# Spatial product of a frequency-routed convolution block: kept pixel-major and added in front of the last projection, star scale folded away

## The chip, the cores and the metric

One Trainium2 chip, one of its cores. The metric is the device time of one execution in microseconds. The kernel before took 259.8 us in the median of three runs (259.14 to 264.2).

## What is computed

The input `x` is 32 images of 128 channels and 16x16 pixels, in fp32. A first block multiplies each image's channels by a gate (a small spline network on the channel means). The second block is the one that the change touches. For each image, with z the normalised input:

```python
xp = star_scale * jnp.square(jax.nn.relu(einsum(z, w_pw1))) + star_bias      # pixels x 256
xf = jnp.fft.rfft2(xp)
weight = einsum('bfc,hwf->bhwc', routeing, cw)                   # per image and channel, complex
spatial_weight = einsum('bfc,hwf->bhwc', spatial_routeing, spatial_weights)
xs = jnp.fft.irfft2(xf * weight)
out = xp * spatial_weight + xs
x = x + einsum('bhwm,dm->bhwd', out, w_pw2)
```

`routeing` and `spatial_routeing` are softmaxes over four filters; their logits come from two small convolution branches over z, averaged over the pixels. The transform is done with matmuls: a 128-slot real form of the spectrum, whose even and odd rows see only the sum and the difference of the upper and lower half of the pixels ("folding").

## The kernel before, in words

Everything is written out by hand, engine by engine, with semaphores. PE is TensorE, DVE VectorE, ACT ScalarE, POOL GpSimd, SP the DMA queue. The first 90 us load, normalise and run the branch convolutions (`taps`, L1198), which PE fills. Then comes the image loop, 32 rounds, one image each, with the second half's softmax work laid in between its rounds 0 to 9 (`windows`, `image_sums`, `logits`, `centred`, `routing`, `routing_part`). The end of `windows` and of `image_sums` is followed at once by the next round's first DVE instruction, L988.

What one image i goes through, with the line of the profile:

- PE `expand`: six f16 matmuls into `bank[0]` (L1292). ACT: relu (L584) and square (L588) into `sq_v`. DVE `halves`: scale and bias into `xp` (L988, 128x512), then its even sum and odd difference into the one buffer `eo` (L994, L995, 128x256 each).
- PE `waves_of`: four fp32 matmuls of `eo` with `forward` into `bank[2]` (L1305, 128 columns each; the trace counts two passes of each). ACT copies them to `spec` (L594).
- PE `mix`: four bf16 matmuls of 32 rows that make the slot filter (`bank[4]`) and the pixel filter (`bank[3]`) of the image (L1334). ACT copies the pixel filter to `swt` (L600).
- PE `turn_pixels`: four fp32 transposes of `xp` to channel-major, into `bank[5]` (in the trace L1106, the line of the helper `turn`). DVE `spatial`: `qt` = `bank[5]` times `swt` (L1014).
- DVE `terms`: `spec` times the slot filter, into `t_re` and `t_im` (L1005, L1006 and the small L1007). POOL `products`: their difference and sum into `prod` (L420, L421, 128x256 each).
- PE `reduce`: four fp32 matmuls of `prod` with `pw2_t` (L1359); ACT copies to `y_sb` (L612). PE `compose`: two fp32 matmuls of `qt` with `pw2_t`, 256 columns each, into `bank[6]` (L1371), then two of `y_sb` with `inverse` (L1378); ACT copies these to `folded` in two instructions (L618, L620).
- POOL `unfold`: sum and difference of `folded` into `waves` (L430, L431), then `waves` added to `x_all` (L436). DVE `finish`: `x_all` times its coefficient plus `bank[6]` (L1018). SP stores the image.

The order of a round is fixed on every engine. PE in round i: expand(i+2), waves_of(i+1), turn_pixels(i+1), mix(i+1), every second round `turn_route` (L1348), reduce(i), compose(i). DVE: halves(i+2), terms(i+1), spatial(i+1), finish(i). POOL: products(i), unfold(i-1), with a wait in `unfold` that looks a round ahead on another engine:

```python
                pool.wait_ge(folded_ready, 2 * i + 2)
                if ahead:
                    pool.wait_ge(eo_ready, 2 * i + 8)
```

So POOL begins image i's `waves` only after DVE has written `eo` of image i+3. The last image is treated apart: DVE itself makes its products (L1090, L1091), and its spatial and spectral parts are added up in `bank[6]` before one last add (L1098).

Of the kernel before, what the change touches and what calls it, by code (L numbers as in the profile page):

```python
# [40 lines left out]
P = 128  # L41
# [121 lines left out]
def build(nc, x, early, kan2, later, sym, branch_r, branch_s, out):  # L163
    ctx = ExitStack()
    with ctx:
# [17 lines left out]
        def of(tensor, pack, name):  # L183
# [77 lines left out]
        relu_v, sq_v = (sb(name, [P, 512])[:, :] for name in ("relu_v", "sq_v"))  # L261

        route = sb("route", [P, 2, P], BF16)
        eo, swt, qt = (sb(name, [P, 2, 256])[:, :, :] for name in ("eo", "swt", "qt"))
        xp = [sb(f"xp{n}", [P, 2, 256])[:, :, :] for n in range(2)]
# [6 lines left out]
        t_last = z32[:, :, :].rearrange("p k s -> p (k s)").rearrange("p (c m a s) -> p c m a s", c=2, m=2, a=2)  # L272

        bank = [ps(f"bank{n}", [P, 512])[:, :] for n in range(8)]
        mixed_slot = bank[4].rearrange("p (m a s) -> p m a s", m=2, a=2)
        mixed_pixel = bank[3].rearrange("p (m s) -> p m s", m=2)
# [24 lines left out]
        v_done, relu_ready, sq_ready, xp_ready, eo_ready = (sem(n) for n in (  # L301
            "v_done", "relu_ready", "sq_ready", "xp_ready", "eo_ready"))
        dft_done, xt_done, w_done, spec_ready, sw_ready = (sem(n) for n in (
            "dft_done", "xt_done", "w_done", "spec_ready", "sw_ready"))
        terms_ready, prod_ready, qt_ready, y_done, y_ready = (sem(n) for n in (
            "terms_ready", "prod_ready", "qt_ready", "y_done", "y_ready"))
        inverse_ready, x_scaled, last_ready = sem("inverse_ready"), sem("x_scaled"), sem("last_ready")
        sp_done, sp_added, folded_done, folded_ready, waves_ready, fin_ready, stored = (sem(n) for n in (
            "sp_done", "sp_added", "folded_done", "folded_ready", "waves_ready", "fin_ready", "stored"))
# [51 lines left out]
        def _(pool):  # L361
# [12 lines left out]
            pool.memset(unused, 0.0).then_inc(rt_zeroed, 1)  # L374
            def places(half, layer):
# [24 lines left out]
            steps.then(pool.tensor_copy(f_res[:, 2:4, :], sw_nat))  # L400
# [14 lines left out]
            def products(i):  # L415
                pool.wait_ge(terms_ready, 3 * i + 3)
# [6 lines left out]
            def unfold(i, ahead=True, between=None):  # L423

                pool.wait_ge(folded_ready, 2 * i + 2)
                if ahead:
                    pool.wait_ge(eo_ready, 2 * i + 8)
# [4 lines left out]
                if between:  # L432
                    between()
# [19 lines left out]
        def _(act):  # L453
# [189 lines left out]
            def round_of(i, pair, j, between=None):  # L643
# [3 lines left out]
                if j == 0:  # L647
                    route_copy(pair + 1)
# [877 lines left out]
```

## Time and profile before

| | |
|---|---|
| Median of three runs | 259.8 us (259.14 to 264.2) |
| Span of the profiled execution, first to last instruction | 257.2 us |
| Granted TensorE clock over the span | 1.000 |
| PE busy | 240.7 us, 94% of the span |
| DVE busy | 194.2 us, 76% |
| ACT busy | 161.1 us, 63% |
| POOL busy | 108.9 us, 42% |
| DMA, mean over the span | 51 GB/s |

The page gives the profiled execution by its span, 257.2 us; its own time is not listed apart, so the 2.6 us up to the median stand for what lies around the span. Of the chain of waits that ended last, 70% is PE and 11% DVE. All times below are microseconds from the span's start. On DVE and POOL an instruction can start before the record of the one ahead has ended; the step from start to start is then what the engine spends on it, and the full duration counts only where somebody waits for the result. DMA issues lie in the first 15 us and, one store an image, in the loop.

### The profile page before, as it was taken

What the parts mean: (1) busy time and instruction counts of PE and PEld (TensorE: products, weight loads), DVE (VectorE), ACT (ScalarE), POOL (GpSimd) and SP (SyncE); (2) the same over time, 40 slices, a digit from 0 to 9 for tenths busy, and PEclk for the clock granted to TensorE, in tenths of its full rate; (3) what the DMA queues carried; (4) which work ended last, traced back from release to release, by engine and by line L of the source; (5) the groups of instructions that cost most, each with busy time, mean ns of one, the idle gap of its engine ahead of it and who ended that gap; (6) DMA issues with size and microseconds to landing.
All of it is one profiled execution on the core that took longest, in us unless ns stands there. A gap on an engine that the chain in (4) does not pass through costs nothing.

```text
span 257.2 us, 6874 instructions
## 1 busy us (share of the span) xinstructions
PE 240.7 (94%) x2225; PEld 187.7 (73%) x2225; DVE 194.2 (76%) x548; ACT 161.1 (63%) x380; POOL 108.9 (42%) x197
## 2 busy tenths in 40 slices
PE   0697799999999999999999999999999999999995
PEld 0686765554545555886988889988888888888984
DVE  3988999955939626996779998858767768768773
ACT  2034586645976748755676677676676676676772
POOL 2422440120000002257455665765665665665663
PEclk9999999999999999999999999999999999999999
DMA  7999200000000000001010010010010010010002
GB/s 212 364 326 348 105 3 3 1 4 3 0 3 0 3 0 0 4 23 35 9 43 20 23 42 24 20 43 20 20 43 20 20 41 20 20 41 20 23 20 82
DMA packets 9483, 13.19 MB, mean 51 GB/s; under 512 B 732, under 2 KB 8924, under 8 KB 9332
## 3 DMA queue, kind: packets, MB, share of 16 engines
q1 hardware_dynamic: 9428, 12.80, 15.3%
q8 instruction: 15, 0.25, 0.4%
q10 hardware_dynamic: 32, 0.08, 0.2%
q14 instruction: 8, 0.07, 0.1%
HBM read 8.69 MB, written 4.19 MB: 50 GB/s over the span
## 4 chain that ended last, share of the span: by engine, by line
PE 70%; DVE 11%; issue 8%; POOL 4%; DMA 3%; ACT 2%; SPq 1%; POOLq 0%; DVEq 0%; ACTq 0%
PE bank L1198 19%; PE bank L1359 10%; PE bank L1305 8%; PE bank L1371 8%; PE bank L1292 6%; PE bank L1106 4%; PE bank L1378 4%; PE bank L1334 3%; DMA x_all<-in_x 3%; PE bank L1136 1%; POOL prod L421 1%; PE bank L1263 1%; PE bank L1213 1%; PE bank L1348 1%; DVE stats L726 1%
## 5 line engine op out<-in xcount | busy, mean ns | idle before, releaser
L420 POOL TENSOR_TENSOR prod<-t_re,t_im 128x256 f32<-128x256 f32 x31 | 22.6, 729 | 51.6 <-DVE t_re L1007 51.2
L988 DVE TENSOR_SCALAR xp<-sq_v,later_sb 128x512 f32<-128x512 f32 x32 | 17.6, 550 | 32.2 <-ACT sq_v L588 31.9
L1198 PE MATMUL bank<-z_all,split_h 128*64 128x450 f16 (+2 forms) x320 | 37.4, 374 | 1.0 <-ACT z_all L503 1.0
L1359 PE MATMUL bank<-later_sb,prod 128*128 128x128 f32 x256 | 36.3, 285 | 0.2 <-POOL prod L421 0.2
L430 POOL TENSOR_TENSOR waves<-folded 128x128 f32<-128x128 f32 x31 | 14.1, 455 | 51.1 <-DVE eo L995 47.4
L1305 PE MATMUL bank<-later_sb,eo 128*128 128x128 f32 x256 | 34.2, 276 | 0.4 <-DVE eo L994 0.4
L1359 PEld LDWEIGHTS bank<-later_sb,prod 128*128 128x128 f32 x256 | 31.1, 192 | 3.9 <-POOL prod L421 2.3
L1305 PEld LDWEIGHTS bank<-later_sb,eo 128*128 128x128 f32 x256 | 31.1, 192 | 1.5 <-DVE eo L994 0.7
L1371 PE MATMUL bank<-qt,later_sb 128*128 128x256 f32 x124 | 31.9, 380 | 0.0
L618 ACT ACTIVATE folded<-bank,coef 128x128 f32<-128x128 f32 x31 | 11.4, 367 | 32.5 <-PE bank L1378 26.2
L1198 PEld LDWEIGHTS bank<-z_all,split_h 128*64 128x64 f16 x320 | 17.2, 110 | 16.0 <-issue 3.1
L436 POOL TENSOR_TENSOR x_all<-x_all,waves 128x256 f32 (+1 forms) x31 | 22.6, 728 | 5.8 <-POOL waves L431 4.9
L584 ACT ACTIVATE relu_v<-bank,w_max 128x512 f32<-128x512 f32 x32 | 22.0, 688 | 3.7 <-PE bank L1292 2.6
L1136 PE MATMUL bank<-early_sb 128*128 128x128 f32 x102 | 15.0, 305 | 9.0 <-DMA x_all<-in_x 9.0
L1014 DVE TENSOR_TENSOR qt<-bank,swt 128x512 f32<-128x512 f32 x31 | 21.2, 683 | 2.7 <-PE bank L1371 2.5
L421 POOL TENSOR_TENSOR prod<-t_re,t_im 128x256 f32<-128x256 f32 x31 | 22.8, 734 | 0.0
L1292 PE MATMUL bank<-split_h,z_all 128*128 128x256 f16 x128 | 22.7, 273 | 0.0
L1371 PEld LDWEIGHTS bank<-qt,later_sb 128*128 128x128 f32 x124 | 21.2, 191 | 1.6
L588 ACT ACTIVATE sq_v<-relu_v 128x512 f32<-128x512 f32 x32 | 20.2, 631 | 1.0
L1005 DVE TENSOR_TENSOR t_re<-spec,bank 128x504 f32<-128x504 f32 x31 | 20.8, 671 | 0.0
L1006 DVE TENSOR_TENSOR t_im<-spec,bank 128x504 f32<-128x504 f32 x31 | 20.8, 671 | 0.0
L1136 PEld LDWEIGHTS bank<-early_sb 128*128 128x128 f32 x102 | 13.6, 214 | 9.0 <-issue 9.0
(176 smaller groups left out, 495.2 us busy)
## 6 DMA issues: line engine op xcount, KB each, us to landing
x_all<-in_x SPq DMA_DIRECT2D x8, 512.0 KB, 8.6
out<-x_all SPq DMA_DIRECT2D x32, 128.0 KB, 1.7
sp_t<-in_branch_s SPq DMA_DIRECT2D x1, 2560.0 KB, 15.6
later_sb<-in_later SPq DMA_DIRECT2D x1, 918.5 KB, 8.8
sym_all<-in_sym SPq DMA_DIRECT2D x1, 292.5 KB
early_sb<-in_early SPq DMA_DIRECT2D x1, 278.0 KB, 3.6
rwf_t<-in_branch_r SPq DMA_DIRECT2D x1, 256.0 KB, 11.8
kan_sb<-in_kan ACTq DMA_DIRECT2D x1, 80.8 KB, 3.3
```

The costliest lines, as they stand in the source:

```text
L420: pool.tensor_tensor(prod[:, :, :, 0, :], halved[0][:, :, 0], halved[1][:, :, 1], ALU.subtract).then_inc(prod_ready, 1)
L421: pool.tensor_tensor(prod[:, :, :, 1, :], halved[0][:, :, 1], halved[1][:, :, 0], ALU.add).then_inc(prod_ready, 1)
L436: pool.tensor_tensor(one(x_all, i), one(x_all, i), waves[:, :, :].rearrange("p u s -> p (u s)"), ALU.add).then_inc(fin_ready, 1)
L584: act.activation(relu_v[:, :], bank[0], ACT.Relu, scale=w_max[:, 2:3]).then_inc(relu_ready, 1)
L1005: tt(t_re[:, :, :, 2:P], spec[:, :, :, 2:P], mixed_slot[:, :, 0, 2:P].unsqueeze(2).broadcast_to(wide_shape), ALU.mult).then_inc(terms_read ...
L1014: tt(qt[:, :, :], bank[5].rearrange("p (m s) -> p m s", m=2), swt[:, :, :], ALU.mult).then_inc(qt_ready, 1)
L1136: mm(bank[1][:, 0:P], group, ident, start=True, stop=True)
L1198: last = mm(dst[:, :, rows_out, cols_out], w[:, t, :], pixels(z_all[:, b:b + 2, part, :])[:, :, rows_in, cols_in], start=(n == 0 and t in ...
L1292: last = mm(bank[0][:, t * MED:(t + 1) * MED], z[:, part, cols], w, start=(n == 0), stop=(n == 2))
L1305: last = mm(dst[:, m, :, 64 * odd:64 * odd + 64], eo[:, odd, m * P:(m + 1) * P], forward[:, odd, :, :], start=True, stop=True)
L1359: last = mm(bank[1][:, odd * C:(odd + 1) * C], prod[:, m, odd].rearrange("p a s -> p (a s)"), pw2_t[:, m, :], start=(m == 0), stop=(m == 1))
L1371: last = mm(bank[6][:, 0:HW], pw2_t[:, m, :], qt[:, m, :], start=(m == 0), stop=(m == 1))
```

## The change

1. The product `qt` is made pixel-major: DVE multiplies `xp` (as written, plus a bias) by a pixel filter that `mix` now makes pixel-major, in `bank[4]`, read from PSUM. The four transposes (`turn_pixels`), ACT's copy to `swt`, and the two 256-column matmuls of `compose` are gone.
2. POOL folds `qt` (`fold`: sum and difference into `qt_eo`), PE transforms it with four fp32 matmuls of 128 columns into `bank[5]` (`waves_onto`), and DVE adds `bank[5]` to POOL's `prod` (`add_pixels`) before `reduce`.
3. The final sum is DVE's alone: `finish` adds `waves` to `x_all`; POOL's L436 is gone, and so is the wait `ahead`.
4. The scale is folded: its root goes into ACT's relu scale, its sign into the filters; ACT's square writes `xp` directly, the bias goes into DVE's two instructions, and L988 is gone. `eo` has two buffers.
5. The orders of all four engines are new; `expand` runs three images ahead, `finish` one round behind. The last image runs like the others.

```diff
             def products(i):
-                pool.wait_ge(terms_ready, 3 * i + 3)
+                pool.wait_ge(re_ready, 2 * i + 2)
+                pool.wait_ge(im_ready, i + 1)
...
-            def unfold(i, ahead=True, between=None):
-
+            def fold(i):
+                pool.wait_ge(qt_ready, i + 1)
+                if not isinstance(i, int) or i >= 1:
+                    pool.wait_ge(q_done, i)
+                pool.tensor_tensor(qt_eo[:, 0, :], qt[:, 0, :], qt[:, 1, :], ALU.add).then_inc(q_folded, 1)
+                pool.tensor_tensor(qt_eo[:, 1, :], qt[:, 0, :], qt[:, 1, :], ALU.subtract).then_inc(q_folded, 1)
+
+            def unfold(i):
                 pool.wait_ge(folded_ready, 2 * i + 2)
-                if ahead:
-                    pool.wait_ge(eo_ready, 2 * i + 8)
                 if not isinstance(i, int) or i >= 1:
                     pool.wait_ge(fin_ready, i)
...
-                pool.tensor_tensor(one(x_all, i), one(x_all, i), waves[:, :, :].rearrange("p u s -> p (u s)"), ALU.add).then_inc(fin_ready, 1)
...
+            with pool.Fori(1, NB - 2) as i:
+                unfold(i)
+                fold(i + 2)
+                products(i + 2)
...
+            def square(i, p):
                 act.wait_ge(relu_ready, i + 1)
-                if not isinstance(i, int) or i >= 1:
-                    act.wait_ge(xp_ready, i)
-                act.activation(sq_v[:, :], relu_v[:, :], ACT.Square).then_inc(sq_ready, 1)
+                if not isinstance(i, int) or i >= 2:
+                    act.wait_ge(qt_ready, i - 1)
+                    act.wait_ge(odd_ready, i - 1)
+                act.activation(xp[p].rearrange("p t m -> p (t m)"), relu_v[:, :], ACT.Square).then_inc(sq_ready, 1)
...
             def round_of(i, pair, j, between=None):
-                relu_square(i + 2)
                 spectrum(i + 1)
-                spatial_mix(i + 1)
                 if j == 0:
                     route_copy(pair + 1)
+                y_copy(i)
                 if between:
                     between()
-                y_copy(i)
+                rectified(i + 3)
                 folded_copy(i)
...
+                square(i + 3, 1 - j)
...
+            def even_sum(i, p):
                 dve.wait_ge(sq_ready, i + 1)
...
+                dve.scalar_tensor_tensor(out=eo[p][:, 0, :], in0=xp[p][:, 0, :], scalar=shift_2[:, 0:1], in1=xp[p][:, 1, :],
+                                         op0=ALU.add, op1=ALU.add).then_inc(even_ready, 1)
+                tt(eo[p][:, 1, :], xp[p][:, 0, :], xp[p][:, 1, :], ALU.subtract).then_inc(odd_ready, 1)
+
+            def spatial(i, p):
+                dve.wait_ge(pixel_done, i + 1)
+                if not isinstance(i, int) or i >= 1:
+                    dve.wait_ge(q_folded, 2 * i)
+                dve.scalar_tensor_tensor(out=qt[:, :, :], in0=xp[p], scalar=shift[:, 0:1], in1=mixed_pixel,
+                                         op0=ALU.add, op1=ALU.mult).then_inc(qt_ready, 1)
...
+            def add_pixels(i):
+                dve.wait_ge(q_done, i + 1)
+                dve.wait_ge(prod_ready, 2 * i + 2)
+                flat = prod[:, :, :, :, :].rearrange("p m o a s -> p (m o a s)")
+                tt(flat, flat, bank[5], ALU.add).then_inc(total_ready, 1)
...
             def finish(i):
-                dve.wait_ge(sp_done, i + 1)
+                dve.wait_ge(waves_ready, 2 * i + 2)
...
-            def round_of(i, p):
-                halves(i + 2, p)
+            def round_of(i, p, between=None):
+                add_pixels(i)
+                even_sum(i + 2, p)
+                spatial(i + 1, 1 - p)
+                if between:
+                    between()
                 terms(i + 1)
-                spatial(i + 1)
-                finish(i)
+                if not isinstance(i, int) or i >= 1:
+                    finish(i - 1)
...
+            def waves_onto(i):
...
+                for odd in range(2):
+                    pe.wait_ge(q_folded, 2 * i + 1 + odd)
+                    for m in range(2):
+                        last = mm(bank[5][:, (2 * m + odd) * P:(2 * m + odd + 1) * P], qt_eo[:, odd, m * P:(m + 1) * P], forward[:, odd, :, :],
+                                  start=True, stop=True)
+                last.then_inc(q_done, 1)
...
             def reduce(i):
...
-                pe.wait_ge(prod_ready, 2 * i + 2)
+                pe.wait_ge(total_ready, i + 1)
...
+                waves_onto(i)
+                if not isinstance(i, int) or i >= 1:
+                    waves_of(i + 1, 1 - j)
                 mix(i + 1, pair + j, 1 - j)
                 if j == 0:
                     turn_route(pair + 1, half)
...
                 reduce(i)
...
+                expand(i + 3)
+                if not between:
+                    compose(i, pair + 2)
```

How the order of instructions moves, at the two places that matter. First POOL, two images of the loop before; L420 and L421 are `products`, L430 and L431 the `waves` of `unfold`, L436 its add to `x_all`:

```order
L420 TENSOR_TENSOR prod<-t_re,t_im 128x4x64
L421 TENSOR_TENSOR prod<-t_re,t_im 128x4x64
L425 ISA
L427 REGISTER_ALU
L430 TENSOR_TENSOR waves<-folded 128x128
L431 TENSOR_TENSOR waves<-folded 128x128
L436 ISA
L436 TENSOR_TENSOR x_all<-x_all,waves 128x256
```

And POOL's whole loop body after, one image (L438 and L439 are `fold`, in front of the products):

```order
L445 TENSOR_TENSOR waves<-folded 128x128
L446 TENSOR_TENSOR waves<-folded 128x128
L435 REGISTER_ALU
L437 REGISTER_ALU
L438 TENSOR_TENSOR qt_eo<-qt 128x256
L439 TENSOR_TENSOR qt_eo<-qt 128x256
L426 ISA
L431 TENSOR_TENSOR prod<-t_re,t_im 128x4x64
L432 TENSOR_TENSOR prod<-t_re,t_im 128x4x64
L455 REGISTER_ALU
L455 COMPARE_AND_BRANCH
```

The add to `x_all` has left POOL, and two folds of 256 columns stand between an image's `waves` and the next products. Next DVE, one image of the loop before:

```order
L988 TENSOR_SCALAR xp0<-sq_v,later_sb 128x512
L994 TENSOR_TENSOR eo<-xp0 128x256
L995 TENSOR_TENSOR eo<-xp0 128x256
L1005 TENSOR_TENSOR t_re<-spec,bank4 128x4x126
L1006 TENSOR_TENSOR t_im<-spec,bank4 128x4x126
L1007 TENSOR_TENSOR t_re<-spec,bank4 128x4x2
L1014 TENSOR_TENSOR qt<-bank5,swt 128x512
L1018 SCALAR_TENSOR_TENSOR x_all<-x_all,coef,bank6 128x256
```

And one image of DVE's loop after, beginning with `add_pixels` (L1027):

```order
L1027 TENSOR_TENSOR prod<-prod,bank5 128x512
L1001 SCALAR_TENSOR_TENSOR eo1<-xp1,shift_2 128x256
L1003 TENSOR_TENSOR eo1<-xp1 128x256
L1009 SCALAR_TENSOR_TENSOR qt<-xp0,shift,bank4 128x512
L1019 TENSOR_TENSOR t_re<-spec,bank3 128x4x126
L1020 TENSOR_TENSOR t_re<-spec,bank3 128x4x2
L1021 TENSOR_TENSOR t_im<-spec,bank3 128x4x126
L1031 SCALAR_TENSOR_TENSOR x_all<-x_all,coef,waves 128x256
```

The first instruction now reads what POOL makes of the instructions above it in the round before; the spatial product stands ahead of the terms, and `finish` reads both inputs from SBUF where it read one from PSUM.

## Rows read from the trace of the kernel before

**Rows 1.** Page, busy time: engine, microseconds, share of the span, instructions.

```profile
PE 240.7 (94%) x2225; PEld 187.7 (73%) x2225; DVE 194.2 (76%) x548; ACT 161.1 (63%) x380; POOL 108.9 (42%) x197
```

**Rows 2.** Timeline, DVE `finish` of images 10 and 28 (start, duration, engine, line).

```profile
157.23 0.47 DVE L1018 SCALAR_TENSOR_TENSOR x_all<-x_all,coef,bank 128x256 f32<-128x256 f32 x1
...
243.55 0.47 DVE L1018 SCALAR_TENSOR_TENSOR x_all<-x_all,coef,bank 128x256 f32 x1
```

**Rows 3.** Timeline, PE in one round of the loop.

```profile
209.23 0.38 PE L1292 MATMUL bank<-split_h,z_all 128*128 128x256 f16 x2
...
209.88 1.06 PE L1305 MATMUL bank<-later_sb,eo 128*128 128x128 f32 x8
210.78 0.60 PE L1106 MATMUL bank<-early_sb,xp 128*128 128x128 f32 x4
211.31 0.39 PE L1334 MATMUL bank<-filters,route 32*128 32x256 bf16 x4
...
212.75 1.03 PE L1371 MATMUL bank<-qt,later_sb 128*128 128x256 f32 x4
213.62 0.64 PE L1378 MATMUL bank<-later_sb,y_sb 128*128 128x128 f32 x4
```

**Rows 4.** Timeline, DVE in one round of the loop.

```profile
207.44 0.43 DVE L994 TENSOR_TENSOR eo<-xp 128x256 f32<-128x256 f32 x1
207.78 0.42 DVE L995 TENSOR_TENSOR eo<-xp 128x256 f32<-128x256 f32 x1
208.12 0.67 DVE L1005 TENSOR_TENSOR t_re<-spec,bank 128x504 f32<-128x504 f32 x1
...
208.71 0.67 DVE L1006 TENSOR_TENSOR t_im<-spec,bank 128x504 f32<-128x504 f32 x1
...
209.30 0.15 DVE L1007 TENSOR_TENSOR t_re<-spec,bank 128x8 f32<-128x8 f32 x1
...
209.37 0.68 DVE L1014 TENSOR_TENSOR qt<-bank,swt 128x512 f32<-128x512 f32 x1
...
209.97 0.47 DVE L1018 SCALAR_TENSOR_TENSOR x_all<-x_all,coef,bank 128x256 f32 x1
```

**Rows 5.** Timeline, POOL in the loop, and the DVE instruction that released it.

```profile
213.24 0.45 POOL L430 TENSOR_TENSOR waves<-folded 128x128 f32<-128x128 f32 x1 [1.80 <-DVE eo L995]
...
247.54 0.15 DVE L1007 TENSOR_TENSOR t_re<-spec,bank 128x8 f32<-128x8 f32 x1
247.78 0.72 POOL L420 TENSOR_TENSOR prod<-t_re,t_im 128x256 f32<-128x256 f32 x1 [0.33 <-DVE t_re L1007]
...
248.46 0.73 POOL L421 TENSOR_TENSOR prod<-t_re,t_im 128x256 f32<-128x256 f32 x1
```

**Rows 6.** Timeline, places where DVE and POOL both read SBUF.

```profile
44.66 0.49 POOL L383 TENSOR_TENSOR k_rel<-k_dist,k_inv 128x176 f32<-128x176 f32 x1 [9.36 <-DVE k_dist L781]
44.85 0.51 DVE L785 SCALAR_TENSOR_TENSOR k_bas<-k_dist,k_ge 128x176 f32<-128x176 f32 x1
...
106.12 0.74 POOL L421 TENSOR_TENSOR prod<-t_re,t_im 128x256 f32<-128x256 f32 x1
106.26 0.62 DVE L890 TENSOR_TENSOR win<-win,cols_sum 128x8 f32<-128x8 f32 x1
```

**Rows 7.** Groups by shape, POOL: count, busy us, mean ns of one.

```profile
L383 POOL TENSOR_TENSOR k_rel<-k_dist,k_inv 128x160 f32<-128x160 f32 x2 | 1.1, 554 | 0.0
```

**Rows 8.** Timeline, PE and DVE where the loop begins and where it ends.

```profile
98.27 0.39 PE L1334 MATMUL bank<-filters,route 32*128 32x256 bf16 x4
...
104.02 0.67 DVE L1005 TENSOR_TENSOR t_re<-spec,bank 128x504 f32<-128x504 f32 x1
...
246.37 0.67 DVE L1005 TENSOR_TENSOR t_re<-spec,bank 128x504 f32<-128x504 f32 x1
...
254.60 0.42 DVE L1098 TENSOR_TENSOR x_all<-x_all,bank 128x256 f32<-128x256 f32 x1 [2.09 <-PE bank L1468]
```

**Rows 9.** Timeline, the first DVE instruction behind `windows`.

```profile
107.80 0.54 DVE L988 TENSOR_SCALAR xp<-sq_v,later_sb 128x512 f32<-128x512 f32 x1
```

More of the change, by code:

```diff
@@ L374, in _ @@
             pool.memset(unused, 0.0).then_inc(rt_zeroed, 1)
+            pool.wait_ge(in_later, 16)
+            steps.then(pool.tensor_scalar(sign_01[:, :], star[:, 0:1], 0.0, None, ALU.is_ge))
+            pool.tensor_scalar(sign[:, :], sign_01[:, :], 2.0, -1.0, ALU.mult, ALU.add).then_inc(sign_set, 1)
+            pool.wait_ge(sign_set, 1)
+            pool.tensor_tensor(size[:, :], star[:, 0:1], sign[:, :], ALU.mult).then_inc(sign_set, 1)
+            steps.then(pool.tensor_tensor(shift[:, :], star[:, 1:2], sign[:, :], ALU.mult))
+            pool.tensor_scalar(shift_2[:, :], shift[:, :], 2.0, None, ALU.mult).then_inc(sign_set, 1)
             def places(half, layer):
@@ L399, in _ @@
             pool.wait_ge(in_later, 16)
-            steps.then(pool.tensor_copy(f_res[:, 2:4, :], sw_nat))
+            pool.wait_ge(sign_set, 1)
+            steps.then(pool.tensor_scalar(f_res[:, 2:4, :], sw_nat, sign[:, 0:1], None, ALU.mult))
             for part in range(3):
@@ L494, in _ @@
             sigmoid_sum(0, 1)
-            ahead(ACT.Sqrt)
+            act.wait_ge(sign_set, 2)
+            act.activation(root[:, :], size[:, :], ACT.Sqrt).then_inc(root_set, 1)
             deviation(0, 2)
@@ L1048, in _ @@
             round_of(3, 1)
-            halves(6, 0)
-            logits(1)
-            terms(5)
-            spatial(5)
-            finish(4)
+            round_of(4, 0, lambda: logits(1))
             centred(1)
@@ L1327, in mix @@
+                last.then_inc(q_done, 1)
+            def mix(i, pair, j, branches=(0, 1)):
                 pe.wait_ge(rt_out, pair + 1)
                 if not isinstance(i, int) or i >= 1:
[L1329 to L1335 removed]
@@ L1338, in turn_route @@
+                if 0 in branches:
+                    pixel.then_inc(pixel_done, 1)
+                if 1 in branches:
+                    slot.then_inc(slot_done, 1)
             def turn_route(n, half):
@@ L1363, in compose @@
             def compose(i, turned_routes):
-                pe.wait_ge(qt_ready, i + 1)
-                if isinstance(i, int) and i == 3:
-                    pe.wait_ge(copied, 3)
-                if not isinstance(i, int) or i >= 1:
-                    pe.wait_ge(sp_added, i)
-                for m in range(2):
-                    last = mm(bank[6][:, 0:HW], pw2_t[:, m, :], qt[:, m, :], start=(m == 0), stop=(m == 1))
-                last.then_inc(sp_done, 1)
                 pe.wait_ge(y_ready, i + 1)
@@ L1398, in _ @@
             expand(1)
+            mix(0, 0, 0, (0,))
             taps(7, 2, 5)
```

322 lines of the change are left out of this document (125 added, 197 removed).

## The prediction

> **What bounds the kernel now.** I read first the page's busy times. The reader should see one engine that is nearly always at work: PE with 94% of the span, against 76% for DVE, 63% for ACT and 42% for POOL [rows 1]. The branch convolutions ahead of the image loop are not touched, so the question is the length of a round. Between the `finish` of image 10 and that of image 28 lie 18 rounds in 86.32 us [rows 2], which is 4.80 us a round. PE's rows of one round follow on one another without a hole [rows 3]: PE sets 4.80. The other engines wait for it once a round.
>
> Two durations matter later. On DVE the reader should look at steps from start to start: 0.34 for a sum of 256 columns, 0.59 for one of 504, 0.60 for one of 512 with an input in PSUM, whose full duration is 0.68 [rows 4]. On POOL a two-input instruction of 256 columns lasts 0.73 and the next one starts 0.68 after it; one of 128 columns lasts 0.45 [rows 5]. DVE's last term ends at 247.69 and POOL starts at 247.78, so a release costs 0.09 [rows 5].
>
> **PE's part of the change.** The four transposes go: from 210.78 to 211.31, 0.53. The two wide matmuls of `compose` go: from 212.75 to 213.62, 0.87. `waves_onto` comes, four fp32 matmuls of 128 columns just like `waves_of`, which take 209.88 to 210.78, 0.90 [rows 3]. The mix keeps its four matmuls of 256 columns. PE's work falls by 0.50, to 4.30 us a round. ACT loses its copy to `swt` and waited for PE anyway, so that is worth nothing by itself, nor is the gone L988: DVE was idle beside it.
>
> **What is late next.** The change closes a ring between DVE and POOL that was not there. DVE, in order, does add_pixels(i), two halves, spatial(i+1), terms(i+1), finish(i-1), and then add_pixels(i+1). That last one waits for POOL's products(i+1), and in POOL's order these stand behind fold(i+1), which waits for DVE's spatial(i+1). So a round cannot be shorter than this path, step by step:
>
> - add_pixels, 512 columns from SBUF and PSUM, start to start 0.60 as L1014 to L1018 [rows 4];
> - the even sum 0.36 and the odd difference 0.34. The odd one is L995. The even one has the three-operand form, which the trace shows only with PSUM: 0.47 against 0.42 for the plain form [rows 4]. Bounds 0.34 and 0.39;
> - the spatial product to its end, 0.73: 0.68 as L1014, and 0.05 for its three-operand form. Bounds 0.68 and 0.78, since this form at 512 columns is in no row;
> - the release to POOL, 0.09;
> - two folds and two products of 256 columns, three steps of 0.68 and one full 0.73, together 2.77 [rows 5];
> - the release from POOL to DVE, in no row; 0.06, between 0 and 0.1.
>
> The sum is 4.95. A second path over terms(i+1) instead of the folds is shorter: spatial 0.60 from start to start, terms 0.59, 0.07 and 0.67, release 0.09, products 1.41, release 0.06, with the 1.30 ahead of them 4.79. POOL's own work is only some 3.6 a round, so neither engine looks full; it is the alternation that costs. PE, 4.30, gets holes.
>
> **What the two engines do to each other.** In the rows of the spline layer both read SBUF together. POOL's L383 runs 44.66 to 45.15; DVE's L785, two inputs in SBUF, starts at 44.85 and takes 0.51 [rows 6], ending 0.21 behind POOL's end, which is about its 176 columns at one each 1.04 ns (0.60 minus 0.34 over 256 columns, [rows 4]). It stood until POOL was done. L890, with 8 columns, takes 0.62 and ends at 106.88, when POOL's L421 has ended at 106.86 [rows 6]. POOL pays less: its next L383, of only 160 columns, lasts 0.55 where the 176-column one took 0.49 [rows 6, 7], some 0.10 too long by its size, that is DVE's 0.18 of reading less a start-up of 0.08. Now `finish` reads `x_all` and `waves`, both in SBUF (before, one was in PSUM), and it is issued some 3.2 after add_pixels starts, in the middle of the folds and products that the ring runs through. By the same measure 256 columns hold POOL for 0.27 less 0.08, 0.19. The halves fall beside the end of the waves (L445, L446), worth 0.01 or so. I take 0.20: a round of 5.15. Bounds are 0 and the whole 0.47 of `finish`.
>
> The Trainium skill says more on this (SBUF — State Buffer, Who interferes with whom): a VectorE instruction with two SBUF inputs and a GpSimd instruction that reads SBUF shut each other out, and the second to issue is blocked until the first has finished. On DVE's side the trace agrees (L785, L890); on POOL's side the 0.10 is less than a whole instruction. Taken whole it gives the third case below.
>
> **Sum.** Before, from terms(1) at 104.02 to terms(30) at 246.37 [rows 8], 29 rounds take 142.35, so 3.2 more than 29 times 4.80: the softmax work of the second half. After:
>
> - 29 rounds at 5.15: 149.4.
> - Softmax work: the 3.2 again, since what PE and DVE do there stays (the free 1.3 us of DVE between `finish` and the products hides it as the idle time did before). But `windows`, 1.54 us from 106.26 to 107.80 [rows 6, 9], reads SBUF twice per small instruction and now falls on the folds and products: most of it must stand until POOL is done, some 1.0 late; the same for `image_sums`; four more places at 0.25 each. Together 6.2 (bounds 3.2 and 7.5).
> - Loop: 155.6 against 142.35, +13.2.
> - Start: the slot half of mix(0), at 98.27 [rows 8], now stands behind expand(2), 0.65, and waves_of(1), 0.90 [rows 3], and behind the pixel half issued apart. Terms(1) comes 1.9 later (bounds 1.0 and 2.2).
> - End: before, from terms(30) at 246.37 to the end of the last add, 254.60 plus 0.42, 8.65 [rows 8]; DVE made the last products itself. After, along the ring: terms(30) to add_pixels(30) 3.15, then 0.60 and 0.73 to the end of the last spatial product, 0.09, four POOL instructions 2.77 plus 0.19, release and add_pixels 0.74, then reduce, copy and the last matmuls 2.55 (four matmuls at 128 columns 0.90 as L1305 and two at 256 columns 0.87 as L1371 [rows 3], 0.78 estimated for the copy between and three releases), add 0.47: 11.3. That is +2.6.
>
> The star scale adds five tiny POOL instructions at 14 us and four on DVE near 60 us; POOL waits for DVE at the one place and PE fills the other, so zero, at most 0.5. It all comes to +17.7: a span of 274.9. With the 2.6 outside the span, as before, 277.5 us.
>
> **Rivals.**
>
> 1. The ring without the lock: finish fits between POOL's instructions. 29 times 4.95 and 3.2 is 146.75, +4.4; start 1.9, end 2.4; +8.7: 268.5 us. For it: POOL's solo rows vary by little. Against: L890 and L785 waited.
> 2. The lock taken whole: POOL loses the full 0.47 per round. 5.42 by 29 is 157.2, with 6.2 it is +21.0; start 1.9, end 2.9: 285.6 us. Against it the 0.55 of L383.
> 3. PE stays the bound, and the change pays: 4.30 by 29 is 124.7, with 3.2 it is -14.5, start +1.9, end 0: 247.2 us. For it: PE's 94% and 0.50 less work. It decides as soon as POOL's four instructions take less than 2.77 minus 0.65, 2.12 together (0.53 each), or DVE's order leaves the ring open. Every POOL row of 256 columns says 0.73, and the order is read off the program, so I give it little.
> 4. Every size at its lowest: spatial 0.68, even 0.34, releases 0.07 less, no lock: 4.81 a round, +0.3; start 1.0, end 2.0: 263.1 us, which is no difference.
>
> **How the numbers follow.** Forecast 0.60, rival 1 0.20, rival 2 0.11, rival 3 0.04, rival 4 0.05. The measurement can tell about 2% from no change, 5.2 us, so the border is at 265.0 above and 254.6 below. Forecast, 1 and 2 lie above it, 0.91; of that I move 0.01 to the middle for what I may have left out. Slower 0.90, same 0.06, faster 0.04. The range leaves out rivals 3 and 4 and the upper part of 2: 267 to 286.
>
> **What would show it.** In the profile after: DVE's add_pixels (L1027) idle in front, released by POOL's second product (L432), once a round and about 1.2 long; rounds of about 5.15; PE's share near 85% with holes ahead of L1357 and L1312; L1031 (`finish`) longer than 0.47, because it stands behind a fold; L431 longer than 0.73. If L1031 reads 0.47, it is rival 1; if L431 reads 1.1 and more, rival 2. If rounds measure 4.3 and DVE does not wait for POOL, the ring is wrong and so is the sign.

## The result and the profile after

The changed kernel takes 280.15 us (median, 279.78 to 280.35), the one before, run beside it, 260.06: a ratio of 1.079 (95% interval 1.076 to 1.081). Forecast were 277.5 us and a slower kernel. The span of the profiled execution is 278.2, against 257.2. Executions of one kernel can differ by up to 5 us (259.14 to 264.2 before), so the experiments below are compared by the length of their rounds as well as by their time.

The page of the kernel after: busy times, the chain that ended last by engine, and the two groups of section 5 that matter most.

```profile
PE 247.6 (89%) x2225; PEld 186.3 (67%) x2225; DVE 209.5 (75%) x549; ACT 146.7 (53%) x348; POOL 139.0 (50%) x237
...
PE 51%; DVE 34%; issue 6%; POOL 3%; DMA 2%; ACT 1%; DVEq 1%; POOLq 1%; SPq 0%; ACTq 0%
...
L1357 PE MATMUL bank<-later_sb,prod 128*128 128x128 f32 x256 | 37.4, 290 | 12.7 <-DVE prod L1027 11.8
L1027 DVE TENSOR_TENSOR prod<-prod,bank 128x512 f32<-128x512 f32 x32 | 22.0, 686 | 34.8 <-POOL prod L432 31.9
```

PE has gone from 94% [rows 1] to 89%, and a third of the chain now runs over DVE. The last line is the shape of the answer: `add_pixels` (L1027) stands idle 34.8 us in all, nearly all of it for POOL's second product, L432. No engine is over 90% busy any more, and the kernel takes 20 us more.

One round of the loop on DVE and POOL, after (start, duration, and in brackets the idle time ahead and who ended it). It answers to [rows 4, 5].

```profile
204.58 0.69 DVE L1027 TENSOR_TENSOR prod<-prod,bank 128x512 f32<-128x512 f32 x1 [1.30 <-POOL prod L432]
...
205.19 0.48 DVE L1001 SCALAR_TENSOR_TENSOR eo<-xp,shift 128x256 f32<-128x256 f32 x1
...
205.58 0.41 DVE L1003 TENSOR_TENSOR eo<-xp 128x256 f32<-128x256 f32 x1
205.92 0.74 DVE L1009 SCALAR_TENSOR_TENSOR qt<-xp,shift,bank 128x512 f32<-128x512 f32 x1
206.57 0.67 DVE L1019 TENSOR_TENSOR t_re<-spec,bank 128x504 f32<-128x504 f32 x1
206.81 0.72 POOL L438 TENSOR_TENSOR qt_eo<-qt 128x256 f32<-128x256 f32 x1 [1.44 <-DVE qt L1009]
...
207.50 0.73 POOL L439 TENSOR_TENSOR qt_eo<-qt 128x256 f32<-128x256 f32 x1
207.83 0.69 DVE L1031 SCALAR_TENSOR_TENSOR x_all<-x_all,coef,waves 128x256 f32 x1
208.19 0.91 POOL L431 TENSOR_TENSOR prod<-t_re,t_im 128x256 f32<-128x256 f32 x1
...
209.07 0.71 POOL L432 TENSOR_TENSOR prod<-t_re,t_im 128x256 f32<-128x256 f32 x1
...
209.81 0.69 DVE L1027 TENSOR_TENSOR prod<-prod,bank 128x512 f32<-128x512 f32 x1 [1.30 <-POOL prod L432]
```

Read it as one ring. DVE runs add, halves, spatial product without a gap (204.58 to 206.66), POOL takes over at 206.81 and runs folds and products without a gap to 209.78, DVE starts again at 209.81. Each engine waits about 1.3 to 1.4 for the other, once a round: 5.23 in all. `finish` at 207.83 lies across a fold, lasts 0.69 and not 0.47, and the product behind it (208.19) lasts 0.91 and not 0.73.

### The profile page after: what moved, and what is told of

Same layout as the page of the kernel before. It is cut to its first block, busy times and chain, and to the rows that moved or that the text cites. A ratio compares the mean times of both kernels' runs of the same rounds, so it can differ in the third digit from the quotient of the medians.

```text
span 278.2 us, 6918 instructions
## 1 busy us (share of the span) xinstructions
PE 247.6 (89%) x2225; PEld 186.3 (67%) x2225; DVE 209.5 (75%) x549; ACT 146.7 (53%) x348; POOL 139.0 (50%) x237
## 4 chain that ended last, share of the span: by engine, by line
PE 51%; DVE 34%; issue 6%; POOL 3%; DMA 2%; ACT 1%; DVEq 1%; POOLq 1%; SPq 0%; ACTq 0%
PE bank L1191 18%; PE bank L1357 6%; PE bank L1312 6%; PE bank L1299 5%; DVE qt L1009 4%; DVE t_re L1019 4%; DVE t_im L1021 4%; DVE prod L1027 4%; PE bank L1286 4%; DVE x_all L1031 3%; POOL prod L432 3%; PE bank L1368 3%; DMA x_all<-in_x 2%; DVE eo L1001 2%; PE bank L1326 2%
## 5 line engine op out<-in xcount | busy, mean ns | idle before, releaser
L438 POOL TENSOR_TENSOR qt_eo<-qt 128x256 f32<-128x256 f32 x32 | 23.3, 727 | 94.1 <-DVE qt L1009 94.1
L1357 PE MATMUL bank<-later_sb,prod 128*128 128x128 f32 x256 | 37.4, 290 | 12.7 <-DVE prod L1027 11.8
L1027 DVE TENSOR_TENSOR prod<-prod,bank 128x512 f32<-128x512 f32 x32 | 22.0, 686 | 34.8 <-POOL prod L432 31.9
L1357 PEld LDWEIGHTS bank<-later_sb,prod 128*128 128x128 f32 x256 | 31.3, 192 | 19.2 <-DVE prod L1027 17.4
L1312 PE MATMUL bank<-later_sb,qt_eo 128*128 128x128 f32 x256 | 41.7, 295 | 0.3
L1312 PEld LDWEIGHTS bank<-later_sb,qt_eo 128*128 128x128 f32 x256 | 33.4, 192 | 7.2 <-issue 2.8
L612 ACT ACTIVATE spec<-bank 128x512 f32<-128x512 f32 x32 | 19.1, 598 | 31.7 <-PE bank L1299 31.0
L1299 PE MATMUL bank<-later_sb,eo 128*128 128x128 f32 x256 | 33.9, 275 | 0.0
L625 ACT ACTIVATE y_sb<-bank 128x256 f32<-128x256 f32 x32 | 12.3, 384 | 37.6 <-PE bank L1357 37.6
L1299 PEld LDWEIGHTS bank<-later_sb,eo 128*128 128x128 f32 x256 | 31.1, 192 | 0.4 <-issue 0.4
L431 POOL TENSOR_TENSOR prod<-t_re,t_im 128x256 f32<-128x256 f32 x32 | 28.7, 898 | 2.1 <-DVE t_im L1021 1.3
L598 ACT ACTIVATE relu_v<-bank,relu_scale 128x512 f32<-128x512 f32 x32 | 22.0, 688 | 12.1 <-PE bank L1286 12.1
L1009 DVE SCALAR_TENSOR_TENSOR qt<-xp,shift,bank 128x512 f32<-128x512 f32 x32 | 23.7, 741 | 0.0
L439 POOL TENSOR_TENSOR qt_eo<-qt 128x256 f32<-128x256 f32 x32 | 23.3, 729 | 0.0
L432 POOL TENSOR_TENSOR prod<-t_re,t_im 128x256 f32<-128x256 f32 x32 | 23.2, 724 | 0.0
L1129 PE MATMUL bank<-early_sb 128*128 128x128 f32 x102 | 15.0, 304 | 9.1 <-DMA x_all<-in_x 9.1
L1368 PE MATMUL bank<-later_sb,y_sb 128*128 128x128 f32 x124 | 21.9, 300 | 1.0 <-ACT y_sb L625 0.9
```

The lines of the kernel that those rows point to most:

```text
L431: pool.tensor_tensor(prod[:, :, :, 0, :], halved[0][:, :, 0], halved[1][:, :, 1], ALU.subtract).then_inc(prod_ready, 1)
L432: pool.tensor_tensor(prod[:, :, :, 1, :], halved[0][:, :, 1], halved[1][:, :, 0], ALU.add).then_inc(prod_ready, 1)
L1009: dve.scalar_tensor_tensor(out=qt[:, :, :], in0=xp[p], scalar=shift[:, 0:1], in1=mixed_pixel, op0=ALU.add, op1=ALU.mult).then_inc(qt_ready, 1)
L1027: tt(flat, flat, bank[5], ALU.add).then_inc(total_ready, 1)
L1299: last = mm(dst[:, m, :, 64 * odd:64 * odd + 64], eo[p][:, odd, m * P:(m + 1) * P], forward[:, odd, :, :], start=True, stop=True)
L1312: last = mm(bank[5][:, (2 * m + odd) * P:(2 * m + odd + 1) * P], qt_eo[:, odd, m * P:(m + 1) * P], forward[:, odd, :, :], start=True, stop ...
```

## Experiments

Rounds are counted from one add_pixels to the next, in the rolled loop.

**e1, the lock of `finish`.** From round 10 on `finish` adds a PSUM bank in place of `waves`; the waves are left out of the result.

```diff
-            def finish(i):
+            def finish(i, psum=False):
                 dve.wait_ge(waves_ready, 2 * i + 2)
+                added = bank[6][:, 0:HW] if psum else waves[:, :, :].rearrange("p u s -> p (u s)")
...
-                                         in1=waves[:, :, :].rearrange("p u s -> p (u s)"), op0=ALU.mult, op1=ALU.add).then_inc(fin_ready, 1)
+                                         in1=added, op0=ALU.mult, op1=ALU.add).then_inc(fin_ready, 1)
```

> The changed kernel, but from round 10 on the last sum of each image reads an unused PSUM bank in place of the waves, so it has one SBUF input as before the change; the waves of those images are left out of the result. Lock theory: the first product on GpSimd falls from 0.91 to 0.73, finish from 0.69 to 0.47, and each of some 19 rounds gets 0.2 shorter, 5.23 to 5.03: 276.3 us. Rival (the first product is slow because of its operands or the loop, not because VectorE reads): products and rounds stay, 280 us.

276.07 us, ratio 1.061 (1.058 to 1.064); rounds 5.05 to 5.06. The same place of the round in e1:

```profile
206.34 0.47 DVE L1032 SCALAR_TENSOR_TENSOR x_all<-x_all,coef,bank 128x256 f32 x1
206.70 0.73 POOL L431 TENSOR_TENSOR prod<-t_re,t_im 128x256 f32<-128x256 f32 x1
```

With one of its inputs in PSUM, `finish` takes 0.47 beside a working POOL and POOL's product 0.73. So the 0.22 more on DVE and the 0.18 on POOL come from the second SBUF input, and the round gives back just POOL's part, 0.18. The lock is shown, at the size forecast.

**e2, no folds.** POOL's two folds are left out, and PE transforms the unfolded product. DVE's next spatial product then waits for that transform in place of the folds.

```diff
-                pool.tensor_tensor(qt_eo[:, 0, :], qt[:, 0, :], qt[:, 1, :], ALU.add).then_inc(q_folded, 1)
-                pool.tensor_tensor(qt_eo[:, 1, :], qt[:, 0, :], qt[:, 1, :], ALU.subtract).then_inc(q_folded, 1)
```

> The changed kernel without GpSimd's two folds; TensorE transforms the unfolded halves, so the spatial part of the result is wrong in that it lacks the fold. GpSimd loses 1.38 us of the 3.65 that it works a round. Ring theory: the path over the folds goes, and the next one, over the terms and the products, ends only 0.15 to 0.35 earlier: rounds of 4.9 to 5.1, about 273 us. Rival (rounds are long because GpSimd has more work): the whole 1.38 is saved until TensorE is the bound at 4.4: 254 us.

278.14 us in the median of four (277.88, 278.52, 278.4 and 274.04), where about 273 were expected; rounds 5.02 to 5.03, as expected. Taking 1.4 us of POOL's work out of a round shortens it by only 0.2: the path over the three terms to the two products is next. POOL now waits for the last term:

```profile
207.66 0.67 DVE L1011 TENSOR_TENSOR t_im<-spec,bank 128x504 f32<-128x504 f32 x1
208.25 0.48 DVE L1021 SCALAR_TENSOR_TENSOR x_all<-x_all,coef,waves 128x256 f32 x1
208.41 0.90 POOL L431 TENSOR_TENSOR prod<-t_re,t_im 128x256 f32<-128x256 f32 x1 [2.61 <-DVE t_im L1011]
209.28 0.72 POOL L432 TENSOR_TENSOR prod<-t_re,t_im 128x256 f32<-128x256 f32 x1
...
210.03 0.69 DVE L1017 TENSOR_TENSOR prod<-prod,bank 128x512 f32<-128x512 f32 x1 [1.30 <-POOL prod L432]
```

The span of that profile, 276.0, fell by 2.2 only, where 29 rounds of 0.2 are 6. The rest was lost ahead of the images: its first add_pixels starts at 107.6 and that of the kernel after at 103.98. PE's preparatory 128-column matmuls (`stir`, L1119 here and L1129 there) took longer per piece between 8 and 24 us. First the kernel after, then e2; behind the count stand busy time and mean ns:

```profile
L1129 PE MATMUL bank<-early_sb 128*128 128x128 f32 x66 | 10.2, 316 | 9.1 <-DMA x_all<-in_x 9.1
```

```profile
L1119 PE MATMUL bank<-early_sb 128*128 128x128 f32 x44 | 10.6, 430 | 8.8 <-DMA x_all<-in_x 8.8
```

In both, 16 that follow on one another take some 3.75 at first, 0.23 each; in the kernel after they then fall to half of that, 0.12 (22 in 2.72 from 21.46 us on), and in e2 they still take 0.23 there (16 in 3.62). The execution of 274.04 has a span of 272.1, which is 6.1 under the kernel after, as the rounds say.

**e3, more work for PE.** Four fp32 transposes of 128 columns more a round, ahead of `reduce`, from round 6 on.

```diff
+                    for n in range(4):
+                        turn(bank[6][:, n * P:(n + 1) * P], ident, P)
                 reduce(i)
```

> The changed kernel with four idle fp32 transposes more on TensorE in every round from 6 on, in front of reduce, 0.53 us a round (what the change took away with turn_pixels); the result stays. Ring theory: TensorE has 0.6 to 0.9 of free time a round, so rounds grow by 0 to 0.15: 280 to 284 us. Rival (TensorE still sets the round): 0.53 by 26 rounds, 294 us.

280.1 us (ratio 1.082, 1.074 to 1.091), rounds 5.24. The matmuls are there (92, four a round in 23 rounds, 0.60 to 0.66 each time; for 23 rounds the rival's 294 would be 292), and the hole ahead of `reduce` shrinks from 12.7 to 6.8:

```profile
PE 253.2 (91%) x2317; PEld 194.2 (70%) x2317; DVE 209.3 (75%) x549; ACT 146.8 (53%) x348; POOL 139.3 (50%) x237
...
L1357 PE MATMUL bank<-later_sb,prod 128*128 128x128 f32 x256 | 35.9, 284 | 6.8 <-DVE prod L1027 6.6
```

PE is not the bound, though its share is again 91%. It is not far from it: it has 69% of the chain that ended last, where it had 51%. But as long as the ring is 5.23, the half microsecond a round that the change took from PE buys nothing.

**e8, both costs at once.** e2's edit and e1's together.

```diff
-                pool.tensor_tensor(qt_eo[:, 0, :], qt[:, 0, :], qt[:, 1, :], ALU.add).then_inc(q_folded, 1)
-                pool.tensor_tensor(qt_eo[:, 1, :], qt[:, 0, :], qt[:, 1, :], ALU.subtract).then_inc(q_folded, 1)
...
-                                         in1=waves[:, :, :].rearrange("p u s -> p (u s)"), op0=ALU.mult, op1=ALU.add).then_inc(fin_ready, 1)
+                                         in1=added, op0=ALU.mult, op1=ALU.add).then_inc(fin_ready, 1)
```

> No folds on POOL (PE transforms the unfolded product) and, from round 10 on, finish reads PSUM in place of waves, so both are left out of the result. If the two costs are independent walls on one path, as I now hold: the round without folds was 5.03 because the path then runs over the three terms and the two products, and finish's lock (0.18 on the first product) is still on it. Taking both gives 4.85 a round and about 270 us (274.0 for the run without folds that had the usual start, less 20 rounds of 0.18). Rival: without folds the lock is no longer on the path (finish then falls beside a product that nobody waits for), rounds stay 5.0 and the time stays at 274.

270.9 us, ratio 1.039 (1.036 to 1.042); rounds 4.85 to 4.86, the forecast to 0.01. The two costs add, since e2's ring still has L431 at 0.90 in it and here it is 0.73. Even without folds and lock the ring between DVE and POOL is longer than the 4.80 of before [rows 2].

### Can another order open the ring?

These runs are read by their rounds first, since two things in their profiles lie ahead of the loop's later rounds and lengthen the time without the ring. In e4, e6, e7 and e11 the first add_pixels starts at 107.07 to 108.12, not at 103.98: from 19 to 24 us, 36 to 40 matmuls fill PE's 5 us as in e2, where 44 take 3.57 in the kernel after. And the granted TensorE clock, 1.00 from 160 to 260 us in every run of this part, is lower in some of the rounds with softmax work: 0.83 from 110 to 120, 120 to 130 and 140 to 150 us in e7, for instance. The kernel after has 0.83 from 100 to 110 us only; e1, whose clock is 1.00 there, has the same first round (6.01 for 6.05).

**e4, one image further ahead.** DVE makes the spatial product of image i+2 behind the terms of i+1; PE's mix is split so that its pixel half comes earlier; POOL's folds also wait until DVE's halves of the next image are done.

```diff
                 even_sum(i + 2, p)
-                spatial(i + 1, 1 - p)
...
                 terms(i + 1)
+                spatial(i + 2, p)
...
-            def fold(i):
+            def fold(i, behind=True):
                 pool.wait_ge(qt_ready, i + 1)
+                if behind:
+                    pool.wait_ge(odd_ready, i + 2)
```

> The changed kernel with the spatial product made one image further ahead (same instructions, other order on VectorE and TensorE), and the folds made to wait for the odd difference of the next image. Ring theory: no path goes through spatial product, folds and products in one round any more; what is left is add_pixels, the halves, the folds and the products on GpSimd, 4.5 to 4.65 a round, near TensorE's own 4.4: 260 to 264 us. Rival (the amount of work, not its order, sets the round): 280 us.

272.98 us, ratio 1.048 (1.044 to 1.052), rounds 4.82 and 4.93 in turn. It is 7 us better than the change as it is, and far from the 260 to 264 expected. The spatial product waited for PE's pixel mix (0.40 <-PE), and `finish` behind it (0.80 on average) was still running when the products had ended: add_pixels then waited for its own engine.

**e6, the pixel mix early, and no wait in the folds.**

```diff
                 reduce(i)
+                mix(i + 2, pair + 1, j, (0,))
...
-                    mix(i + 2, pair + 1, j, (0,))
                     compose(i, pair + 2)
...
-                if behind:
-                    pool.wait_ge(odd_ready, i + 2)
```

> The kernel that runs the spatial product an image further ahead, without the wait that held the folds back, and with PE's pixel mix of image i+2 issued right behind reduce(i), ahead of expand and compose. In the run before it (272.98 us, rounds 4.82 to 4.93) the spatial product waited 0.40 for that mix and finish stood in front of add_pixels. If the late mix was the wall, spatial starts 0.4 to 0.5 earlier, and add_pixels then goes by POOL's second product: rounds of 4.6 to 4.7, 266 to 269 us. Rival: finish's lock with the products is the wall whatever the mix does (finish ends when the product ends, as before): rounds stay at 4.8 to 4.9 and the time at 272 to 273.

279.49 us (1.073, 1.067 to 1.079), rounds 4.97: both theories missed it. The rounds are 0.26 shorter than in the kernel after, and the time is not: in the profile, from the first add_pixels to the last are 164.8 us, where it was 168.1, but the first comes 3.8 later. The group of the odd difference, 180 to 260 us (count, busy, mean ns), e6:

```profile
L1003 DVE TENSOR_TENSOR eo<-xp 128x256 f32<-128x256 f32 x17 | 16.1, 949 | 0.0
```

It takes 418 ns in the kernel after. Without the wait the folds run just when DVE makes the halves: the fold L438 stands behind the even sum, and the odd difference behind the fold.

**e7, the transform ahead too.** As e6, and PE's waves_onto(i+1) is issued behind reduce(i); POOL folds before it unfolds.

```diff
             def round_of(i, pair, j, half=0, between=None):
-                waves_onto(i)
...
                 mix(i + 2, pair + 1, j, (0,))
+                waves_onto(i + 1)
```

> As the last, and also the forward transform of the spatial product runs one image ahead: PE issues waves_onto(i+1) behind reduce(i), so waves_of(i+1) opens the round and its spectrum is there when add_pixels(i) ends; POOL folds before it unfolds. Then nothing in the ring between DVE and POOL is longer than add_pixels 0.6, halves 0.7, terms 1.3, products 1.4 and releases 0.2, 4.2 to 4.4 with locks, and PE's own 4.3 is the bound: rounds 4.35 to 4.5 and 256 to 262 us, about the kernel before or a little under it. Rival: DVE is the wall, since its own work with the locks of two halves and finish is some 4.3 to 4.6 a round and the softmax work of the second half no longer finds idle time: rounds 4.6 to 4.7, 264 to 268 us.

286.24 us (1.099, 1.092 to 1.106), rounds 5.23. The collision is plain in its rows:

```profile
209.20 0.72 POOL L438 TENSOR_TENSOR qt_eo<-qt 128x256 f32<-128x256 f32 x1
209.27 0.69 DVE L1027 TENSOR_TENSOR prod<-prod,bank 128x512 f32<-128x512 f32 x1 [0.61 <-POOL prod L432]
...
209.87 1.02 DVE L1001 SCALAR_TENSOR_TENSOR eo<-xp,shift 128x256 f32<-128x256 f32 x1
209.88 0.72 POOL L439 TENSOR_TENSOR qt_eo<-qt 128x256 f32<-128x256 f32 x1
...
210.56 0.64 POOL L445 TENSOR_TENSOR waves<-folded 128x128 f32<-128x128 f32 x1
210.81 0.67 DVE L1003 TENSOR_TENSOR eo<-xp 128x256 f32<-128x256 f32 x1
211.17 0.63 POOL L446 TENSOR_TENSOR waves<-folded 128x128 f32<-128x128 f32 x1
```

add_pixels reads one input from PSUM and takes its 0.69 beside the fold L438. The even sum, with both in SBUF, stands until fold L439 ends at 210.60 and takes another 0.29: 1.02. Reading, it holds up POOL's L445 in turn (0.64 for 0.45), and the odd difference stands until that one ends at 211.20. From add_pixels to the first term are 2.14 (209.27 to 211.41), where 0.60, 0.39 and 0.34 would do: the 0.8 over is what the deeper order had won.

**e9, e7 and `finish` with PSUM.** e7 with e1's edit. Expected was no difference (within 1 us) if PE is the bound there, and rounds 0.1 to 0.2 shorter and 2 to 5 us less if DVE and its locks are the wall. It took 285.72 us (1.100, 1.086 to 1.113), the same time as e7, but the rounds are 5.05 in place of 5.23: the lock of `finish` is on the path there too, at the same 0.18 as in e1, and PE's 4.3 is not the bound. As in e1 the waves are left out of the result. The halves still collide with POOL (0.92 and 0.67). The time does not show the gain, since rounds with softmax work were longer in this profile (8.95, 11.31 and 8.24, in e7 7.08, 10.77 and 6.93). The granted clock was lower there, 0.66 from 120 to 125 us and 0.62 from 143 to 150 (e7: 0.75 from 122 to 127 and 0.72 from 144 to 150); whether that is all of it is open.

**e11, e10, e12, the wait back in.** e11 is e6 and e10 is e7 with this wait and POOL's order as in e4; e12 is e10 with e1's edit.

```diff
-            def fold(i):
+            def fold(i, behind=True):
                 pool.wait_ge(qt_ready, i + 1)
+                if behind:
+                    pool.wait_ge(odd_ready, i + 2)
...
-                fold(i + 2)
                 unfold(i)
+                fold(i + 2)
```

The moved `fold` is e10's alone (e11 has that order already).

> e6_mix_first with the wait put back that holds POOL's folds until DVE's halves of the next image are done. The last call left that wait out, and the trace shows the price: the even sum and the odd difference, two SBUF inputs each, took about 1.0 and 0.67 there instead of 0.4, since each stands until POOL's instruction beside it is finished. With the wait the halves should read 0.6 or less and rounds fall from 4.97 by 0.2 to 0.35, to 4.65 to 4.75: 267 to 271 us. Rival: the order of PE's mix is what cost there, then rounds stay above 4.9.

275.4 us (1.059, 1.055 to 1.064), rounds 4.86 to 4.87. The two durations in the expectation are those of e7; in e6 the even sum took 0.48 and the odd difference 0.95. With the wait they take 0.78 and 0.41: the odd difference is free, and the even sum now stands beside POOL's L448. The wait is worth 0.11 a round where 0.2 to 0.35 were expected, and there is no gain on e4. In its rows the first fold waits 0.78 for the odd difference, and from there POOL runs its four instructions without a gap; the add comes when `finish`, which ended last, is through (e11's two folds, and the spatial product that waits for the second):

```profile
208.29 0.73 POOL L440 TENSOR_TENSOR qt_eo<-qt 128x256 f32<-128x256 f32 x1 [0.78 <-DVE eo L1008]
...
208.98 0.73 POOL L441 TENSOR_TENSOR qt_eo<-qt 128x256 f32<-128x256 f32 x1
...
209.74 0.75 DVE L1014 SCALAR_TENSOR_TENSOR qt<-xp,shift,bank 128x512 f32<-128x512 f32 x1 [0.36 <-POOL qt_eo L441]
...
210.41 0.96 DVE L1036 SCALAR_TENSOR_TENSOR x_all<-x_all,coef,waves 128x256 f32 x1
```

The wait has put the folds between halves and products again: the same ring, closed at another place.

> e7_transform_ahead with the same wait and POOL's order back to waves, folds, products. Theory: SBUF access shared by DVE's two-SBUF instructions and POOL is the real bound now. POOL's six instructions take 3.7 a round and DVE's three (even, odd, finish) can't read meanwhile, 0.27 each by 1.04 ns a column: 4.5 together. Rounds then come to 4.5 to 4.65 against 5.23, and with the softmax rounds still long (10.8 for one there) 262 to 268 us. Rival: the ring itself (not the collisions) is what holds e7 at 5.23: the wait then changes nothing or makes it longer, 284 us and more.

296.3 us (1.139, 1.135 to 1.143), rounds 5.70 and 5.79: the rival, and worse. Here PE's transform waits for the folds (0.46 <-POOL), `expand` stands behind it, ACT's square behind that, and the even sum waits for it (0.96 <-ACT xp). My budget of shared SBUF access (4.5) is a lower limit that no order came near, not a forecast.

> e10 with finish reading PSUM from round 10 on (the waves are left out of the result). By the budget of shared SBUF access it frees 0.2 to 0.27 a round: 0.15 to 0.25 below e10's rounds, 3 to 5 us less, unless PE's own 4.3 is reached first. Rival: no difference from e10, so finish's access is not on the path there.

299.61 us (1.157, 1.149 to 1.164), rounds 5.70 and 5.79 as in e10: `finish` is not on that ring. In the profiles 1.3 us of the difference from e10 lie in one round of the softmax work (7.04 for 5.71), where the granted clock is 0.83 from 150 to 160 us and 1.00 in e10; the rest is open.

**e13, e7 without folds.** e7 with e2's edit.

```diff
-                fold(i + 2)
                 unfold(i)
                 products(i + 2)
```

> e7_transform_ahead without POOL's folds (PE transforms the unfolded product, so the fold is left out of the result). Three orders so far gave rounds of 4.86 to 5.79, all with two folds and two products in a row between DVE's halves and add_pixels. Theory: it is these 1.4 us of folds, by their own time in the ring or by the halves that stand behind them, that no order hides. Without them the halves read 0.4 to 0.7 again and rounds come to 4.3 to 4.6, 22 to 29 rounds of 0.65 to 0.9 less than e7's 286: 262 to 269 us. Rival: e7's order is bad by itself (DVE's own work and the waits for PE), and then rounds stay above 4.9.

278.23 us in the median of six (274.08 to 279.66), rounds 4.73 and 5.02 in turn, 4.87 on average. Taking the folds out is worth 0.36 a round there and not 0.65 to 0.9; in every second round `finish` (0.88) stands behind a product, and the spatial product waits for PE (0.22 and 0.43 in turn). That the folds are all of the cost in the ahead orders is not shown.

No version beat the kernel before. The best that computes the same is e4, 272.98.

## Why the prediction was right, point by point

- **PE loses its place as the bound.** Right: its share is 89% (85% forecast), it has holes ahead of L1357, and e3 shows that work put back costs nothing. The holes forecast ahead of L1312 are not there (0.3 us idle in all). Its eight passes last 1.30 us and more in most rounds, though, where the same shape in L1299 takes 1.06, so part of the wait for the second fold is probably counted as busy.
- **The ring over DVE and POOL.** Right in its order and nearly in every term. Measured: 0.61, 0.39, 0.34, 0.74, release 0.15, folds 0.69 and 0.69, products 0.88 and 0.71, release 0.03, together 5.23; forecast 5.15. The mis-sized terms are the release from DVE to POOL (0.15, I took 0.09), the even sum 0.39 for 0.36, and the POOL steps 0.69 for 0.68; the release back, 0.03, was taken at 0.06. Over 29 rounds the 0.08 are 2.3 of the 3.3 us by which the span was short. DVE's idle time, 1.30, was forecast at 1.2.
- **The second path.** Forecast at 4.79 beside 4.95; e8, without the lock, measures 4.85, 0.06 over; e2, with it, 5.03. Rival 3 had this wrong: faster POOL instructions in the first path alone would not have made PE the bound, since the second path, over terms and products, is longer than 4.30 too. e2 shows it: with no folds at all the round is still 5.03.
- **The lock.** 0.20 forecast, e1 shows 0.18. Rival 1 (none) and rival 2 (the whole 0.47) are both excluded by the rows: L1031 0.69, L431 0.91. The Trainium skill (SBUF — State Buffer, Who interferes with whom) says that the second to issue is blocked until the first has finished. For DVE behind POOL the rows agree (L1001 in e7). For POOL behind DVE they agree as well, once the wait is counted from POOL's own start: `finish` stood until the fold L439 had ended (208.23) and itself ended at 208.52, and the product had started at 208.19, only 0.33 before that. It was 0.18 late. In e2 0.32 of `finish` were left when the product started, and it took 0.90 for 0.73. The clearest case is in e6, where the even sum is not held up itself (0.48) and 0.40 of it are left:

```profile
184.62 0.48 DVE L1001 SCALAR_TENSOR_TENSOR eo<-xp,shift 128x256 f32<-128x256 f32 x1
184.70 0.98 POOL L438 TENSOR_TENSOR qt_eo<-qt 128x256 f32<-128x256 f32 x1
```

  POOL is 0.25 late there. So what POOL loses, in these three, is the time from its own start to DVE's end, less about 0.15. My 0.20 came from the right lock with another sum (DVE's reading of 0.27 less 0.08): that the sum fits is in part luck, since `finish`, held by the fold, ended 0.31 to 0.33 after the product's start in every round from 160 us on. Rival 2 took the lock as whole, which it is, but priced it at all of `finish`, of which only that last part falls on the product.
- **Softmax work.** The sum is right; of its parts only `windows` was looked at. 158.19 from terms(1) to terms(30) less 29 times 5.23 is 6.5; 6.2 forecast. `windows` alone went from 1.54 to 2.81 (107.22 to 110.03), 1.3 late where I had 1.0; its small instructions stand behind folds and products:

```profile
108.29 0.69 DVE L900 TENSOR_TENSOR win<-win,cols_sum 128x8 f32<-128x8 f32 x1
...
109.26 0.85 DVE L907 TENSOR_TENSOR win<-win,bars 128x8 f32<-128x8 f32 x4
```

- **Start.** terms(1) at 105.97 against 104.02: +1.95, forecast +1.9. The slot half of mix(0) ends at 100.88 and ended at 98.66 before.
- **End.** terms(30) at 264.16 to the end of the last add at 276.07, 11.9; forecast 11.3, before 8.65. The step that was too small is the last one: from `reduce` to the last add I had 2.55 and it is 2.87.

```profile
272.04 0.69 DVE L1027 TENSOR_TENSOR prod<-prod,bank 128x512 f32<-128x512 f32 x1 [1.37 <-POOL prod L432]
...
275.65 0.42 DVE L1091 TENSOR_TENSOR x_all<-x_all,bank 128x256 f32<-128x256 f32 x1 [2.37 <-PE bank L1437]
```

```profile
272.78 1.16 PE L1357 MATMUL bank<-later_sb,prod 128*128 128x128 f32 x8 [1.34 <-DVE prod L1027]
274.51 1.10 PE L1437 MATMUL bank<-inverse_all,y_sb 128*128 128x256 f32 x4 [0.56 <-ACT y_sb L625]
```

  `reduce` lasts 1.16, copy and releases take 0.57, the last four matmuls 1.10, 2.83 in all to 275.61; I had taken steps from start to start (0.90, 0.87) for them, where at the end of a chain the whole duration counts. The other 0.3 lies in the rest of the round ahead (3.31 for 3.15; 0.10 of this is a slip, as my own ring, 5.15 less 0.60, 0.36, 0.34 and 0.60, gives 3.25) and in two releases (0.16 and 0.10 for 0.09 and 0.06).
- **The sum.** +15.8 in the loop, +1.95 and +3.3 are +21.0 on the span; forecast +13.2, +1.9, +2.6, 3.3 less. Outside the span were 1.9 and not 2.6. That makes 280.15 for 277.5.
- **Star scale.** Nothing in these terms is left over for it; it was not run by itself.

## What to carry to other kernels

When a change takes work off the busiest engine, write down the ring that its new dependences close over the other engines, in their program order, with durations and releases. If that ring is longer than the busy engine's round, the saving is lost and the share of no engine tells it. Between DVE and POOL count also which DVE instructions read SBUF twice: they and POOL's work take turns, and an order that puts them side by side to hide one behind the other hides little (in e7 a fold of 0.72 and an even sum of 0.48 take 1.02 together). A path of almost the same length right behind the one you remove (5.03 behind 5.23) means that one edit alone brings little.

## What the hardware showed that I had not expected

- A release from DVE to POOL took 0.15 behind the spatial product (206.66 to 206.81), and 0.16 twice at the end. Back from POOL to DVE it took 0.03 in the rolled loop (idle 1.30) and 0.10 in the unrolled rounds at both ends (idle 1.37), for the same two instructions. Why is open.
- The three-operand form at 512 columns lasts 0.74 against 0.69 for the plain one, and its next instruction starts 0.65 to 0.66 after it.
- A DVE instruction with two SBUF inputs started just beside a POOL instruction of 0.72 took 1.02 at 256 columns in place of 0.48 (e7), while one with an input in PSUM kept its 0.69.
- Start times in the trace don't tell who gets the lock when they are close: in e7 the even sum starts at 209.87 and the fold at 209.88, in e11 the even sum at 207.02 and L448 at 207.06, and it is the even sum that stands both times.
- PE's first matmuls ran at 0.23 each until they dropped to 0.12, and in e2's profile that happened later, with 3.6 us to pay at the first image. The granted clock reads 1.00 in both stretches, so that row did not show it; the durations did.
